# A Mamba scan whose VectorE and GpSimd work goes in pairs of steps, with a new split of the C product between the two

## The chip, the cores and the metric

One core of a Trainium2 chip runs the whole program. The metric is the device time of one execution in microseconds (us), median of the runs. TensorE (PE) multiplies matrices, VectorE (DVE) and GpSimd (POOL) work element by element, ScalarE (ACT) computes activation functions, and SyncE (SP) issues DMAs. Each engine takes its own instructions in program order and waits for the others by semaphores.

## The reference

16 sequences (images cut into 196 patches, and 128 text tokens: L = 324 tokens of H = 192 channels) go through 16 Mamba layers and then through a mixture of 16 experts. The layers are what the change touches:

```python
def mamba_layer(x, p):
    in_w, cw, cb, xp_w, dtw, dtb, a_log, dp, ow, nw = p
    h = rmsnorm(x, nw)
    xz = jnp.einsum('blh,ch->blc', h, in_w)
    u, z = jnp.split(xz, 2, axis=-1)
    u = jax.nn.silu(causal_conv(u, cw, cb))
    proj = jnp.einsum('bli,ci->blc', u, xp_w)
    dt_r, Bm, Cm = (proj[..., :R], proj[..., R:R + N], proj[..., R + N:])
    dt = jax.nn.softplus(jnp.einsum('blr,ir->bli', dt_r, dtw) + dtb)
    A = -jnp.exp(a_log)
    y = selective_scan(u, dt, A, Bm, Cm, dp)   # h = exp(dt*A)*h + dt*u*B;  y = sum over n of h*C, + u*D
    y = y * jax.nn.silu(z)
    return x + jnp.einsum('bli,hi->blh', y, ow)
```

I = 384 channels times N = 16 states give 6144 recurrences over 324 tokens for each sequence and layer.

## The kernel before

A *unit* is one sequence in one layer: 256 units (`UNITS`). A unit's recurrences are cut into 16 *steps* `s`. A step holds 128 partitions times 3 tiles of 324 tokens: 972 elements in each partition. For each step

- ACT writes the decay exp(dt*A) into PSUM (`se_decay`, L646, three instructions, one for each tile). There are two decay buffers, so the decay of step s waits for the scan of step s-2;
- POOL writes dt*u*B into `dbu` (`ge_dbu`, L912), a ring of 4 (`DRING`), so this waits for the scan of step s-4;
- DVE scans (`ve_scan`, L847) into `h`, a ring of 8 (`RING`), so a scan waits for TensorE's sums of the step eight before;
- DVE multiplies `h` by C in place (`ve_product`, L856), which TensorE has spread over the partitions in PSUM (`te_bcast`, L466, once for four steps, one buffer); for the steps in `ON_POOL` = 3, 7 and 12 POOL does it (`ge_product`, L920), from a copy of C in SBUF;
- TensorE sums over the states into `y_ps` (`te_sum`, L479, for two steps at a time).

When the sums of a unit are there, DVE multiplies `y_ps` by silu(z) (`ve_gate`, L864), and TensorE projects the result (`te_out`, L523 and L525). Around this lie, for units further on, the norm (`te_ss` L569, `se_log_ss` L715, `ge_x_norm` L926), the projections (`te_u` L543, `te_z` L508), the convolution (`te_conv` L557), silu (`se_silu` L697 and L703), and dt: `te_dt` L586, then a softplus made of Abs, Relu, Exp, Ln and Identity on ACT and three accumulating DMAs that POOL issues (`ge_dt`, L936 and L940). dt and dt*u go through HBM and come back spread over partitions (`sp_load_dt`, `sp_load_dtu`). All of TensorE's results except the sums and C go through one PSUM bank, `pj`: a projection waits until ACT has copied the one before it out of the bank.

The order of the work is written by hand, one function for each engine (`tensor_step`, `scalar_step`, `vector_step`, `gpsimd_step`, `sync_step`), which stands in a loop of two units. A name such as S5 stands below for the scan of step 5, D5 for its decay and S0' for the scan of step 0 of the next unit.

Of the kernel before, what the change touches and what calls it, by code (L numbers as in the profile page):

```python
# [331 lines left out]

def run_layers(nc, cst, x_T, params, weights, b_rows, dt_rows, dtu_rows):

    ident, ones96, sel_c, fold = cst["ident"], cst["ones96"], cst["sel_c"], cst["fold"]
    with ExitStack() as ctx:
# [110 lines left out]

        def by_vector(u, s):

            if s < 0:
                return by_vector(u - 1, s + N)
            return (N - len(ON_POOL)) * u + sum(i not in ON_POOL for i in range(s + 1)) + 1

        def by_pool(u, s):

            if s < 0:
                return by_pool(u - 1, s + N)
            return len(ON_POOL) * u + sum(i in ON_POOL for i in range(s + 1)) + 1
# [1656 lines left out]
```

## Time and profile before

| | us |
|---|---|
| median of 3 runs | 13945.11 |
| lowest and highest | 13933.89, 13954.32 |
| span of the profiled execution | 13964.1 |
| of it the 256 units | about 12,494 |
| a unit, from one wait of DVE to the next | 48.81 |
| busy in the span: PE, DVE, ACT, POOL | 12204.2, 12892.4, 11365.0, 12631.1 |

The profiled execution's span is its own device time, 19 us (0.14%) above the median. Busy times of DVE and POOL add up records that overlap by a little, since an instruction is recorded as started while the last one's end is still being written; the distance from one start to the next is the real price in a full queue. TensorE's ends are modelled.

### The profile page before, as it was taken

Reading aid. Unit: us, or ns where it says so; the run is one execution under the profiler, and the core shown is the slowest. Engines: PE = TensorE matmul, PEld = TensorE weight load, DVE = VectorE, ACT = ScalarE, POOL = GpSimd, SP = SyncE. Lnnn points to the kernel's source line nnn. Section 1 sums busy time; section 2 is a strip of 40 time slices with the busy share of each in tenths; the row PEclk is TensorE's granted clock in tenths of the full one; section 3 lists DMA queues with packets and bytes.
Section 4 is the critical chain, followed back from the end, with each engine's and each line's share of the span. In section 5 each row is a group of like instructions: output and inputs, shape, how many; then the busy total and the mean of one; then the engine's idle time right before and its main releaser. Section 6 shows DMA issues by size and latency. Waiting matters only on the chain. (4 is left out here: it accounts for less than half of the span.)

```text
span 13964.1 us, 203073 instructions
## 1 busy us (share of the span) xinstructions
PE 12204.2 (87%) x51466; PEld 6379.1 (46%) x51466; DVE 12892.4 (92%) x8757; ACT 11365.0 (81%) x21744; POOL 12631.1 (90%) x6352
## 2 busy tenths in 40 slices
PE   7888888888888888888888888888888888888898
PEld 4444444444444444444444444444444444444776
DVE  2999999999999999999999999999999999997533
ACT  4888888888888888888888888888888888887111
POOL 2999999999999999999999999999999999996033
PEclk8999999999999999999999999999999999999899
DMA  4555555555555555555555555555555555554122
GB/s 104 156 160 157 156 164 161 166 154 161 157 161 161 162 161 155 162 156 165 160 165 155 159 159 156 166 161 163 155 161 156 163 161 161 161 155 128 36 63 52
DMA packets 825576, 2086.15 MB, mean 149 GB/s; under 512 B 101243, under 2 KB 381308, under 8 KB 825336
## 3 DMA queue, kind: packets, MB, share of 16 engines
q1 hardware_dynamic: 693720, 1684.45, 36.0%
q0 software_dynamic: 130992, 399.73, 15.2%
q14 instruction: 114, 0.93, 0.0%
q10 hardware_dynamic: 720, 0.55, 0.0%
q8 instruction: 30, 0.49, 0.0%
HBM read 1414.20 MB, written 286.41 MB: 122 GB/s over the span
## 5 line engine op out<-in xcount | busy, mean ns | idle before, releaser
L912 POOL TENSOR_TENSOR dbu<-dtu_rep,b_rep 128x972 f32<-128x972 f32 x4096 | 9534.2, 2511 | 137.2 <-DVE h L847 109.5
L847 DVE TENSOR_TENSOR_SCAN h<-ps,dbu 128x972 f32<-128x972 f32 x4096 | 8723.4, 2166 | 207.8 <-ACT ps L646 207.8
L646 ACT ACTIVATE ps<-dt_rep,A_cur 128x323 f32<-128x323 f32 x12288 | 5842.5, 520 | 957.0 <-DVE h L847 950.5
L856 DVE TENSOR_TENSOR h<-h,ps 128x972 f32<-128x972 f32 x3329 | 3731.2, 1146 | 0.2 <-DVE ps L1206 0.2
L479 PE MATMUL ps<-h,fold 128*32 128x486 f32 x16400 | 3567.5, 577 | 90.1 <-DVE h L856 89.4
L920 POOL TENSOR_TENSOR h<-h,c_rep 128x972 f32<-128x972 f32 x769 | 1853.0, 2410 | 0.0
L557 PE MATMUL ps<-u_raw,w_cv 128*128 128x162 f32 (+7 forms) x8256 | 1801.5, 372 | 28.6 <-ACT u_raw L682 1.5
L479 PEld LDWEIGHTS ps<-h,fold 128*32 128x32 f32 x16400 | 784.9, 110 | 1961.1 <-issue 1731.1
L557 PEld LDWEIGHTS ps<-u_raw,w_cv 128*128 128x128 f32 x8256 | 1351.6, 190 | 509.4 <-ACT u_pre L689 159.5
L543 PE MATMUL ps<-x_norm,w_u 96*128 96x324 f32 (+1 forms) x4128 | 987.7, 383 | 65.1 <-ACT u_raw L682 55.9
L466 PE MATMUL ps<-c_rows,sel_c 16*128 16x324 f32 x2048 | 827.8, 484 | 209.1 <-DVE h L856 201.2
L508 PE MATMUL ps<-x_norm,w_z 96*128 96x324 f32 (+1 forms) x4112 | 983.5, 383 | 1.4 <-ACT rstd L715 0.7
L525 PE MATMUL ps<-y_gated,w_o 128*96 128x324 f32 x3084 | 925.9, 436 | 0.0
L543 PEld LDWEIGHTS ps<-x_norm,w_u 96*128 96x128 f32 x4128 | 665.7, 191 | 541.1 <-ACT u_raw L682 277.9
L586 PE MATMUL ps<-xp_rows,w_dt 49*128 49x162 f32 (+1 forms) x2064 | 562.1, 393 | 388.7 <-ACT dt L743 207.8
L577 PE MATMUL ps<-u_act,w_x 128*128 128x324 f32 x1548 | 490.2, 453 | 461.8 <-ACT u_act L697 454.8
...
L508 PEld LDWEIGHTS ps<-x_norm,w_z 96*128 96x128 f32 x4112 | 661.1, 190 | 447.0 <-issue 179.5
L466 PEld LDWEIGHTS ps<-c_rows,sel_c 16*128 16x128 f32 x2048 | 299.9, 183 | 834.6 <-DVE h L856 629.8
L586 PEld LDWEIGHTS ps<-xp_rows,w_dt 49*128 49x128 f32 x2064 | 321.0, 187 | 788.0 <-ACT dt L743 429.6
L523 PE MATMUL ps<-x_T,ident 96*96 x1028 | 401.9, 473 | 315.8 <-ACT z_pre L670 201.9
L525 PEld LDWEIGHTS ps<-y_gated,w_o 128*96 128x96 f32 x3084 | 504.5, 164 | 337.0
...
## 6 DMA issues: line engine op xcount, KB each, us to landing
dt_rep<-dt_rows SPq DMA_DIRECT2D x1028, 486.0 KB, 5.6
dtu_rep<-dtu_rows SPq DMA_DIRECT2D x1028, 486.0 KB, 4.8
b_rep<-b_rows SPq DMA_DIRECT2D x1028, 162.0 KB, 5.2
dt<-exp_x POOLq DMA_DIRECT2D x257, 486.0 KB, 5.1
dt<-dtu POOLq DMA_DIRECT2D x257, 486.0 KB, 4.4
dt<-u_pre POOLq DMA_DIRECT2D x257, 486.0 KB, 4.4
dt_rows<-dt SPq DMA_DIRECT2D x257, 486.0 KB, 2.6
dtu_rows<-dtu SPq DMA_DIRECT2D x257, 486.0 KB, 2.6
```

What stands on the lines that cost most here:

```text
L466: pe.matmul(c_ps, sel_c[64:80, q, :], c_rows[par][64:80, :], start=True, stop=True).then_inc(s_cbc, 1)
L479: mm = pe.matmul(y_ps[32 * r:32 * r + 32, half, :], fold[:, :], src[:, half * YW:(half + 1) * YW], start=(m in (0, 1)), stop=(m < 0))
L508: mm = pe.matmul(pj[:, lo:hi], w_z[:, c, it * 128:it * 128 + 128], x_norm[par][:, c, t:t + hi - lo], start=(c == 0), stop=(c == 1))
L525: mm = pe.matmul(pj[0:HC, 0:L], w_o[:, it, half * HC:(half + 1) * HC], y_gated[:, it, :], start=False, stop=(it == IT - 1))
L543: mm = pe.matmul(pj[:, lo:hi], w_u[:, c, it * 128:it * 128 + 128], x_norm[par][:, c, t:t + hi - lo], start=(c == 0), stop=(c == 1))
L557: mm = pe.matmul(pj[:, lo + skip:hi], w_cv[:, it * KC + KC - 1 - back, :], u_raw[:, it * L + t + skip - back:it * L + t + hi - lo - back], ...
L586: mm = pe.matmul(pj[:, lo:hi], w_dt[:, it * 128:it * 128 + 128], xp_rows[0:RB, t:t + hi - lo], start=True, stop=True)
L646: ins = act.activation(decay[s % 2][:, it * L + 1:(it + 1) * L], dt_rep[:, s % NR, it, 1:L], ACT.Exp, scale=A_cur[:, it * N + s:it * N + s ...
L847: dve.tensor_tensor_scan(h[s % RING][:, :, :].rearrange("p i t -> p (i t)"), decay[s % 2], dbu[s % DRING][:, :, :].rearrange("p i t -> p ( ...
L856: dve.tensor_tensor(h[s % RING][:, :, :], h[s % RING][:, :, :], c_ps.unsqueeze(1).broadcast_to([128, IT, L]), ALU.mult).then_inc(s_prod, 1)
L912: pool.tensor_tensor(dbu[s % DRING][:, :, :], dtu_rep[:, r, :, :], b_rep[:, q, :].unsqueeze(1).broadcast_to([128, IT, L]), ALU.mult).then_ ...
L920: pool.tensor_tensor(h[s % RING][:, :, :], h[s % RING][:, :, :], c_rep[:, at, :].unsqueeze(1).broadcast_to([128, IT, L]), ALU.mult).then_i ...
```

## The change

Steps go in pairs. POOL writes `dbu` of two steps by one instruction, and a product with C is one instruction for two steps. POOL now has the product of steps 2 and 3, and of the pair 10 and 11 it takes the first four of the six tiles, while DVE takes the last two; DVE has all other pairs. Each engine's order is written anew, the gate comes behind S1' and waits for all eight sums of its unit, and the pass runs up to five units ahead where it was three. The first memsets of `h`, `z_act` and others go.

```diff
--- before.py
+++ after.py
...
-ON_POOL = (3, 7, 12)
...
-MAIN_SET = "exp_and_others"
+MAIN_SET = "natural_log_exp_and_others"
 LOG_SET = "natural_log"
-FREED = 2 + RING + 1 + 1 + 2 + 1 + 1
+SILU_SET = "silu_and_others"
+FREED = 2
+
+
+DEEP = 5
+
+EXPS = (0, 1, 2, 3, 4, 5, 6, 7, 8, 9, 10, 11, 12, 13, 14, 15)
+SCANS = (0, 1, 2, 3, 4, 5, 6, 7, 8, 9, 10, 11, 12, 13, 14, 15)
+INPUTS = (0, 2, 4, 6, 8, 10, 12, 14)
+PRODUCTS = (0, 4, 6, 8, 10, 12, 14)
+POOL_PRODUCTS = (2, 10)
+SUMS = (0, 2, 4, 6, 8, 10, 14, 12)
+
+ALONE = ()
+SUMMED = 2
+
+SHARED = {10: 4}
+
+
+def turn(order, u, s):
+
+    if s < 0:
+        return turn(order, u - 1, s + N)
+    return len(order) * u + order.index(s) + 1
+
+
+def both(order, u, s):
+
+    if s < 0:
+        return both(order, u - 1, s + N)
+    return turn(order, u, max(s, s + 1, key=order.index))
...
-        def te_sum(pe, u, m):
-
-            reached(pe, s_prod, by_vector(u, 2 * m + 1))
-            if not {2 * m % N, (2 * m + 1) % N}.isdisjoint(ON_POOL):
-                reached(pe, s_pprod, by_pool(u, 2 * m + 1))
-            if m == 0:
-                reached(pe, s_gate, u + 1)
+        def te_sum(pe, u, s):
+
+            if any(at in PRODUCTS for at in range(s, s + SUMMED)):
+                reached(pe, s_prod, turn(PRODUCTS, u, last(PRODUCTS, range(s, s + SUMMED))))
+            if any(at in POOL_PRODUCTS for at in range(s, s + SUMMED)):
+                reached(pe, s_pprod, turn(POOL_PRODUCTS, u, last(POOL_PRODUCTS, range(s, s + SUMMED))))
+            if s < NR:
+                reached(pe, s_gate, u)
             for half in range(2):
-                for s in (2 * m, 2 * m + 1):
-                    r = s % NR
-                    src = h[s % RING][:, :, :].rearrange("p i t -> p (i t)")
-                    mm = pe.matmul(y_ps[32 * r:32 * r + 32, half, :], fold[:, :], src[:, half * YW:(half + 1) * YW],
-                                   start=(m in (0, 1)), stop=(m < 0))
+                for step in range(s, s + SUMMED):
+                    r = step % NR
+                    mm = pe.matmul(y_ps[32 * r:32 * r + 32, half, :], fold[:, :],
+                                   flat(h, step)[:, half * YW:(half + 1) * YW], start=(s < NR),
+                                   stop=(s == last(SUMS, range(s % NR, N, NR))))
             mm.then_inc(s_sum, 1)
...
+                freed = te_dt(pe, v[2], 0, freed)
+            if on[0]:
+                te_sum(pe, v[0], 8)
+            if on[4]:
+                freed = te_ss(pe, v[4], freed)
+            if on[2]:
+                freed = te_dt(pe, v[2], 1, freed)
+            if on[0]:
+                te_sum(pe, v[0], 10)
+            if on[2]:
+                freed = te_z(pe, v[2], q[2], 0, freed)
+            if on[0]:
+                te_sum(pe, v[0], 14)
+            if on[2]:
+                freed = te_z(pe, v[2], q[2], 1, freed)
+            if on[0]:
+                te_sum(pe, v[0], 12)
+                freed = te_out(pe, v[0], 0, freed)
+            if on[1]:
+                te_bcast(pe, v[1], q[1], 0)
+            if on[0]:
+                freed = te_out(pe, v[0], 1, freed)
+            if on[3]:
+                freed = te_u(pe, v[3], q[3], 0, freed)
...
+        def scalar_step(act, u, par):
...
+                se_decay(act, v[0], 12)
+            act.preload_act_table_set(SILU_SET)
+            if on[2]:
+                se_silu_u(act, v[2], q[2])
+            act.preload_act_table_set(MAIN_SET)
+            if on[0]:
+                se_decay(act, v[0], 13)
+            if on[2]:
+                se_xp(act, v[2])
+            if on[0]:
+                se_decay(act, v[0], 14)
+            if on[2]:
+                se_dt(act, v[2], 0)
+            if on[0]:
+                se_decay(act, v[0], 15)
+            if on[1]:
+                se_copy_A(act, v[1])
+            if on[4]:
+                se_log_ss(act, v[4])
+            if on[1]:
+                se_decay(act, v[1], 0)
+            if on[4]:
+                se_copy_nw(act, v[4])
+            if on[2]:
+                se_dt(act, v[2], 1)
+            if on[1]:
+                se_decay(act, v[1], 1)
+            if on[2]:
+                se_exp_x(act, v[2])
+                se_one_plus(act, v[2])
+                se_log(act, v[2])
+                se_z(act, v[2], 0)
+                se_less(act, v[2])
+            if on[1]:
+                se_decay(act, v[1], 2)
+            if on[2]:
+                se_z(act, v[2], 1)
+            if on[3]:
+                se_copy_cb(act, v[3])
+            if on[1]:
+                se_decay(act, v[1], 3)
+            if on[5]:
+                se_sq(act, v[5])
+            if on[1]:
+                se_decay(act, v[1], 4)
+            if on[0]:
+                se_out(act, v[0], 0)
+            if on[2]:
+                se_c_rows(act, v[2], q[2])
+                se_lost(act, v[2])
+            if on[1]:
+                se_decay(act, v[1], 5)
+            if on[0]:
+                se_out(act, v[0], 1)
+            if on[1]:
+                se_decay(act, v[1], 6)
...
         def ve_scan(dve, u, s):
-            reached(dve, s_exp, 16 * u + s + 1)
-            reached(dve, s_dbu, 16 * u + s + 1)
-            if s % 2 == 0:
-                reached(dve, s_sum, 8 * u + s // 2 - 1)
-            dve.tensor_tensor_scan(h[s % RING][:, :, :].rearrange("p i t -> p (i t)"), decay[s % 2],
-                                   dbu[s % DRING][:, :, :].rearrange("p i t -> p (i t)"),
-                                   0.0, ALU.mult, ALU.add).then_inc(s_scan, 1)
+            reached(dve, s_exp, turn(EXPS, u, s))
+            reached(dve, s_dbu, turn(INPUTS, u, s // 2 * 2))
+            reached(dve, s_sum, turn(SUMS, u, s // SUMMED * SUMMED - RING))
+            dve.tensor_tensor_scan(flat(h, s), decay[s % 2], flat(dbu, s), 0.0, ALU.mult, ALU.add).then_inc(s_scan, 1)
 
         def ve_product(dve, u, s):
 
-            if s == min(i for i in range(s // 4 * 4, N) if i not in ON_POOL):
-                reached(dve, s_cbc, 4 * u + s // 4 + 1)
-            reached(dve, s_scan, 16 * u + s + 1)
-            dve.tensor_tensor(h[s % RING][:, :, :], h[s % RING][:, :, :],
-                              c_ps.unsqueeze(1).broadcast_to([128, IT, L]), ALU.mult).then_inc(s_prod, 1)
+            reached(dve, s_cbc, 4 * u + s // NR + 1)
+            n = width(s)
+            reached(dve, s_scan, turn(SCANS, u, last(SCANS, range(s, s + n))))
+            mine = slice(SHARED.get(s, 0), n * IT)
+            dve.tensor_tensor(steps(h, s, n)[:, mine, :], steps(h, s, n)[:, mine, :],
+                              each(c_ps, n)[:, mine, :], ALU.mult).then_inc(s_prod, 1)
 
         def ve_gate(dve, u, par):
 
-            reached(dve, s_sum, 8 * u + 2)
-            reached(dve, s_za, u)
+            reached(dve, s_sum, turn(SUMS, u, SUMS[-1]))
+            reached(dve, s_skip, u + 1)
+            reached(dve, s_za, u + 1)
...
+        def vector_step(dve, u, par):
+
+            v, q, on = pass_of(u, par)
+            if on[0]:
+                ve_scan(dve, v[0], 5)
+                ve_scan(dve, v[0], 6)
+                ve_scan(dve, v[0], 7)
+                ve_product(dve, v[0], 4)
+                ve_product(dve, v[0], 6)
+                ve_scan(dve, v[0], 8)
+                ve_scan(dve, v[0], 9)
+                ve_scan(dve, v[0], 10)
+                ve_scan(dve, v[0], 11)
+                ve_product(dve, v[0], 8)
+                ve_product(dve, v[0], 10)
+                ve_scan(dve, v[0], 12)
+                ve_scan(dve, v[0], 13)
+                ve_scan(dve, v[0], 14)
+                ve_scan(dve, v[0], 15)
+                ve_product(dve, v[0], 12)
+                ve_product(dve, v[0], 14)
+            if on[1]:
+                ve_scan(dve, v[1], 0)
+                ve_scan(dve, v[1], 1)
+            if on[0]:
+                ve_gate(dve, v[0], q[0])
+            if on[1]:
+                ve_scan(dve, v[1], 2)
+                ve_scan(dve, v[1], 3)
+                ve_scan(dve, v[1], 4)
+                ve_product(dve, v[1], 0)
...
-            reached(pool, s_scan, 16 * u + s + 1 - DRING)
-            pool.tensor_tensor(dbu[s % DRING][:, :, :], dtu_rep[:, r, :, :],
-                               b_rep[:, q, :].unsqueeze(1).broadcast_to([128, IT, L]), ALU.mult).then_inc(s_dbu, 1)
+            reached(pool, s_scan, both(SCANS, u, s - DRING))
+            pool.tensor_tensor(steps(dbu, s, 2), steps(dtu_rep, r, 2), each(b_rep[:, q, :], 2), ALU.mult).then_inc(s_dbu, 1)
...
+            at = POOL_PRODUCTS.index(s)
+            wait(pool, s_cr[at], 16 * (u + 1))
+            n = width(s)
+            reached(pool, s_scan, turn(SCANS, u, last(SCANS, range(s, s + n))))
+            mine = slice(0, SHARED.get(s, n * IT))
+            pool.tensor_tensor(steps(h, s, n)[:, mine, :], steps(h, s, n)[:, mine, :],
+                               each(c_rep[:, at, :], n)[:, mine, :], ALU.mult).then_inc(s_pprod, 1)
...
+        def gpsimd_step(pool, u, par):
+
+            v, q, on = pass_of(u, par)
+            if on[0]:
+                ge_product(pool, v[0], 2)
+            if on[1]:
+                ge_add(pool, v[1], 2)
+            if on[0]:
+                ge_dbu(pool, v[0], 8)
+                ge_dbu(pool, v[0], 10)
+            if on[1]:
+                ge_dtu(pool, v[1], q[1])
+            if on[0]:
+                ge_dbu(pool, v[0], 12)
+                ge_dbu(pool, v[0], 14)
+            if on[3]:
+                ge_x_norm(pool, v[3], q[3])
+            if on[0]:
+                ge_product(pool, v[0], 10)
+            if on[1]:
+                ge_dbu(pool, v[1], 0)
+                ge_dbu(pool, v[1], 2)
+            if on[2]:
+                ge_add(pool, v[2], 0)
+            if on[1]:
+                ge_dbu(pool, v[1], 4)
+            if on[2]:
+                ge_add(pool, v[2], 1)
+            if on[1]:
+                ge_dbu(pool, v[1], 6)
...
+        def sync_step(sp, u, par, due=()):
...
+                sp_load_dtu(sp, v[1], 0)
+                sp_load_dt(sp, v[1], 0)
+                sp_load_dtu(sp, v[1], 1)
+                sp_load_dt(sp, v[1], 1)
+            if on[2]:
+                sp_store_b(sp, v[2], q[2])
+            if on[1]:
+                sp_load_dtu(sp, v[1], 3)
+                sp_load_dt(sp, v[1], 2)
+                sp_load_c(sp, v[1], q[1], 0)
+                sp_load_dtu(sp, v[1], 2)
...
```

How the order of instructions changes is shown at two places. The first is on TensorE (PE), around the last sums of a unit. L479 (now L528) is `te_sum`, L508 (now L560) `te_z`, L466 `te_bcast`, and L523 (now L571) is the start of `te_out`. Before:

```order
L466 MATMUL ps<-c_rows,sel_c 128x324 [waits s_prod]
L62 ISA
L508 MATMUL ps<-x_norm,w_z 128x324 [waits s_lnss,s_wz]
L508 MATMUL ps<-x_norm,w_z 128x324
L508 MATMUL ps<-x_norm,w_z 128x162 x2
L479 MATMUL ps<-h,fold 32x486 [waits s_prod]
L479 MATMUL ps<-h,fold 32x486 x3
L79 ISA
L508 MATMUL ps<-x_norm,w_z 128x162 [waits s_zev]
L508 MATMUL ps<-x_norm,w_z 128x162
L508 MATMUL ps<-x_norm,w_z 128x324 x2
L62 ISA [waits s_gate]
```

Now, on TensorE at the same place:

```order
L78 REGISTER_ALU
L528 MATMUL ps<-h,fold 32x486 [waits s_prod]
L528 MATMUL ps<-h,fold 32x486 x3
L560 MATMUL ps<-x_norm,w_z 128x162 [waits s_zev]
L560 MATMUL ps<-x_norm,w_z 128x162
L560 MATMUL ps<-x_norm,w_z 128x324 x2
L78 REGISTER_ALU
L528 MATMUL ps<-h,fold 32x486 [waits s_prod]
L528 MATMUL ps<-h,fold 32x486 x3
L571 ISA [waits s_wo,s_gate,s_zev]
L571 MATMUL ps<-x_T,ident 96x324
L573 MATMUL ps<-y_gated,w_o 96x324 x3
```

Before, the unit's last sum (L479) stood ahead of the second half of z and was the last thing that the gate needed. Now two sums stand on the two sides of that half: steps 14 and 15 first, then z, then steps 12 and 13, and both are needed by the gate.

The second place is on GpSimd (POOL), around the product of the middle pair. L912 (now L997) is `ge_dbu`, L920 (now L1006) the product, L926 (now L949) the norm, L940 `dtu`. Before:

```order
L926 TENSOR_TENSOR x_norm<-x_norm,rstd 96x648 [waits s_xw,s_rstd]
L79 REGISTER_ALU
L912 TENSOR_TENSOR dbu<-dtu_rep,b_rep 128x972 [waits s_scan]
L79 REGISTER_ALU
L912 TENSOR_TENSOR dbu<-dtu_rep,b_rep 128x972 [waits s_scan]
L62 ISA
L79 REGISTER_ALU [waits s_acc]
L940 TENSOR_TENSOR dtu<-dt,u_act 128x972 [waits s_ua]
L920 TENSOR_TENSOR h<-h,c_rep 128x972 [waits s_scan,s_cr1]
L79 REGISTER_ALU [waits s_bq3]
L912 TENSOR_TENSOR dbu<-dtu_rep,b_rep 128x972 [waits s_scan]
```

Now, on GpSimd:

```order
L949 TENSOR_TENSOR x_norm<-x_norm,rstd 96x648 [waits s_xw,s_rstd]
L1006 TENSOR_TENSOR h<-h,c_rep 128x1296 [waits s_scan,s_cr1]
L61 ISA
L78 REGISTER_ALU [waits s_bq0,s_dur1,s_dur0]
L997 TENSOR_TENSOR dbu<-dtu_rep,b_rep 128x1944 [waits s_scan]
L78 REGISTER_ALU [waits s_dur3,s_dur2]
L997 TENSOR_TENSOR dbu<-dtu_rep,b_rep 128x1944 [waits s_scan]
L78 REGISTER_ALU
L78 ISA [waits s_less]
L61 ISA [waits s_dtev]
L1017 DMA dt<-exp_x 128x972 [waits s_acc]
```

Every `dbu` instruction now holds 1944 elements in a partition instead of 972, waits for the second scan of a pair, and needs two of the replicated `dtu_rep` blocks at once; the shared product (1296 elements) stands right behind the norm.

## Rows read from the trace of the kernel before

**Rows 1.** Windows: PE, PEld, DVE, ACT, POOL busy us; then clock, DMA share, GB/s.

```profile
281.00:12775.00 12494.00, 10952.26 (x45534) 5433.33 (x45534) 12355.49 (x7669) 11032.55 (x20981) 12353.44 (x6139) 1.00 0.54 160
5999.54:6048.35 48.81, 42.78 (x180) 21.25 (x178) 48.33 (x31) 43.13 (x83) 48.32 (x25) 1.00 0.53 158
...
12790.00:12794.00 4.00, 2.79 (x10) 0.65 (x12) 3.31 (x4) 0.00 (x0) 0.00 (x0) 0.73 1.01 350
```

**Rows 2.** The timeline of DVE in a unit: start, length, and idle time before.

```profile
5999.54 6.33 DVE L847 TENSOR_TENSOR_SCAN h<-ps,dbu 128x972 f32<-128x972 f32 x3 [0.48 <-ACT ps L646]
6005.79 3.29 DVE L856 TENSOR_TENSOR h<-h,ps 128x972 f32<-128x972 f32 x3
6009.00 4.25 DVE L847 TENSOR_TENSOR_SCAN h<-ps,dbu 128x972 f32<-128x972 f32 x2
...
6014.22 1.16 DVE L864 TENSOR_TENSOR y_gated<-ps,z_act 128x972 f32<-128x972 f32 x1
6015.30 2.17 DVE L847 TENSOR_TENSOR_SCAN h<-ps,dbu 128x972 f32<-128x972 f32 x1
```

**Rows 3.** The timeline of POOL in the same unit.

```profile
6017.55 2.25 POOL L912 TENSOR_TENSOR dbu<-dtu_rep,b_rep 128x972 f32<-128x972 f32 x1 [0.40 <-DVE h L847]
...
6027.94 2.53 POOL L912 TENSOR_TENSOR dbu<-dtu_rep,b_rep 128x972 f32<-128x972 f32 x1
6030.14 1.84 POOL L926 TENSOR_TENSOR x_norm<-x_norm,rstd 96x648 f32<-96x648 f32 x1
...
6040.48 9.07 POOL L912 TENSOR_TENSOR dbu<-dtu_rep,b_rep 128x972 f32<-128x972 f32 x4
6049.32 2.43 POOL L920 TENSOR_TENSOR h<-h,c_rep 128x972 f32<-128x972 f32 x1
6051.52 6.85 POOL L912 TENSOR_TENSOR dbu<-dtu_rep,b_rep 128x972 f32<-128x972 f32 x3
```

**Rows 4.** The timeline of ACT in the same unit.

```profile
6000.81 0.56 ACT L742 ACTIVATE exp_x<-ps 128x486 f32<-128x486 f32 x1
...
6001.76 1.44 ACT L646 ACTIVATE ps<-dt_rep,A_cur 128x323 f32<-128x323 f32 x3
...
6004.18 1.01 ACT L749 ACTIVATE exp_x<-exp_x 128x972 f32<-128x972 f32 x1
6005.10 2.79 ACT L646 ACTIVATE ps<-dt_rep,A_cur 128x323 f32<-128x323 f32 x6
6007.91 1.28 ACT L778 ACT_TABLE_LOAD   x1
...
6009.64 1.09 ACT L753 ACTIVATE dtu<-exp_x,one 128x972 f32<-128x972 f32 x1
...
6019.28 1.11 ACT L757 ACTIVATE u_pre<-exp_x,one 128x972 f32<-128x972 f32 x1
...
6042.72 1.48 ACT L697 ACTIVATE u_act<-u_pre,cb_cur 128x324 f32<-128x324 f32 x3
```

**Rows 5.** The page's DMA issues: size of one and us to landing.

```profile
dtu_rep<-dtu_rows SPq DMA_DIRECT2D x1028, 486.0 KB, 4.8
```

**Rows 6.** The timeline of PE around the sums ahead of the gate.

```profile
6005.39 1.33 PE L569 MATMUL ps<-sq,ones 96*96 96x324 f32 x4
...
6009.14 0.81 PE L466 MATMUL ps<-c_rows,sel_c 16*128 16x324 f32 x2 [0.25 <-DVE h L856]
6009.88 1.90 PE L508 MATMUL ps<-x_norm,w_z 96*128 96x324 f32 x8
6011.71 1.82 PE L479 MATMUL ps<-h,fold 128*32 128x486 f32 x8
6013.47 1.91 PE L508 MATMUL ps<-x_norm,w_z 96*128 96x162 f32 x8
```

**Rows 7.** The last unit's end: sums on PE, the gate on DVE.

```profile
12791.21 4.88 PE L479 MATMUL ps<-h,fold 128*32 128x486 f32 x16 [1.53 <-DVE h L856]
...
12796.14 1.17 DVE L864 TENSOR_TENSOR y_gated<-ps,z_act 128x972 f32<-128x972 f32 x1 [2.83 <-PE ps L479]
```

More of the change, by code:

```diff
@@ L325, in _, with width, last, runs @@
                             root((g - 1) * NG + i)
-MAIN_SET = "exp_and_others"
+MAIN_SET = "natural_log_exp_and_others"
 LOG_SET = "natural_log"
-FREED = 2 + RING + 1 + 1 + 2 + 1 + 1
+SILU_SET = "silu_and_others"
[18 more added lines that the diff above has]
+    return turn(order, u, max(s, s + 1, key=order.index))
+def width(s):
+    return 1 if s in ALONE else 2
+def last(order, steps):
+    return max((s for s in order if s in steps), key=order.index)
+def runs(u, ahead):
+    return not isinstance(u, int) or u + ahead >= 0
 def run_layers(nc, cst, x_T, params, weights, b_rows, dt_rows, dtu_rows):
@@ L446, in pick, with flat, steps, each @@
             return table[:, la * width:(la + 1) * width] if isinstance(la, int) else table[:, bass.ds(la * width, width)]
[L449 to L459, printed above, removed]
+        def flat(ring, s):
+            return ring[:, s % ring.shape[1], :, :].rearrange("p i t -> p (i t)")
+        def steps(ring, s, n):
+            at = s % ring.shape[1]
+            return ring[:, at:at + n, :, :].rearrange("p s i t -> p (s i) t")
+        def each(rows, n):
+            return rows.unsqueeze(1).broadcast_to([128, n * IT, L])
         def te_bcast(pe, u, par, q):
@@ new lines, in se_exp_x, with se_log, se_one_plus @@
+        def se_exp_x(act, p):
+            reached(act, s_dtev, 2 * p + 2)
+            act.activation(exp_x[:, :], exp_x[:, :], ACT.Exp, scale=-1.0).then_inc(s_e, 1)
+        def se_log(act, p):
+            reached(act, s_e, p + 1)
+            wait(act, s_dst[1], 16 * p)
+            act.activation(dtu[:, :], exp_x[:, :], ACT.Ln, bias=cst["one"][:, 0:1]).then_inc(s_l, 1)
+        def se_one_plus(act, p):
+            reached(act, s_e, p + 1)
+            reached(act, s_ua, p + 1)
+            wait(act, s_acc, 48 * p)
+            act.activation(u_pre[:, :], exp_x[:, :], ACT.Identity, bias=cst["one"][:, 0:1]).then_inc(s_one, 1)
@@ L762, in se_c_rows, with se_lost, se_less @@
+        def se_lost(act, p):
+            reached(act, s_one, p + 1)
+            act.activation(u_pre[:, :], u_pre[:, :], ACT.Identity, bias=cst["one"][:, 0:1], scale=-1.0).then_inc(s_lost, 1)
+        def se_less(act, p):
+            reached(act, s_one, p + 1)
+            reached(act, s_l, p + 1)
+            act.activation(exp_x[:, :], exp_x[:, :], ACT.Identity, bias=less[:, 0:1]).then_inc(s_less, 1)
         def se_c_rows(act, p, par):
@@ L1094, in early @@
         def early(step, eng):
-            step(eng, -3, 1, scan=False, a1=False, b1=False)
-            step(eng, -2, 0, scan=False, b1=False)
-            step(eng, -1, 1, scan=False)
+            for u in range(-DEEP, 0):
+                step(eng, u, u % 2)
         def all_units(step, eng):
             early(step, eng)
-            with eng.Fori(0, UNITS // 2) as pair:
+            with eng.Fori(0, UNITS // 2) as two:
                 for par in range(2):
-                    step(eng, 2 * pair + par, par)
+                    step(eng, 2 * two + par, par)
```

689 lines of the change are left out of this document (254 added, 435 removed).

## Prediction

> **What bounds the kernel now.** I read the windows first [rows 1]. The reader should see that two engines are near the top at once: the 256 units take 12,494 us, 48.8 us each, and inside one unit of 48.81 us DVE is busy 48.33, POOL 48.32, ACT 43.13 and PE 42.78, with the granted clock of TensorE at 1.00, its 2.4 GHz level. So the kernel is one long steady state: whatever changes a unit by 0.1 us changes the time by 26 us, and everything before and behind the units is as it was, but for some memsets and the filling of the pipeline.
>
> Then the timelines, for the price of an instruction in a full queue, which is the distance between starts. On DVE [rows 2] three scans take 6005.79 - 5999.54 = 6.25, so a scan (S) is 2.083 us; three products take 6009.00 - 6005.79 = 3.21, so one is 1.07; the gate is 6015.30 - 6014.22 = 1.08. The only wait of DVE in a unit is 0.48, for ACT. On POOL [rows 3] I go by ends: a `dbu` is (6.85 + 6051.52 - 2.43 - 6049.32)/3 = 2.207, say 2.20; the product behind four of them ends 2.20 after them; the norm (648 elements) ends 1.51 after the `dbu` before it. POOL waits 0.40 for a scan; the rest of the unit, 48.81 - 20 x 2.20 - 1.51 - 0.40 = 2.9, is its three DMA issues.
>
> **What the change does to each sum.** DVE: still 16 scans, 33.33 us. 13 products become six of 1944 elements and one of 648. No row shows a product of 1944. With no fixed part a pair is 2 x 1.07 = 2.14; with a fixed part as large as the overlap of records (3.29 - 3.21 = 0.08) it is 2.06. I take 2.06, since every short instruction of the trace costs more for an element than a long one, and 0.73 for the 648 elements. With the gate: 33.33 + 12.36 + 0.73 + 1.08 = 47.50 (47.4 to 47.9), against 48.33. If nothing waited, the unit would be 1.3 us shorter.
>
> POOL: the trace has no instruction of 1944 elements. From 648 and 972 elements, (2.20 - 1.51)/324 = 2.13 ns for an element and 0.13 us fixed; a pair is 4.27, the shared product of 1296 elements 2.89. Sum: eight `dbu` and one product of 4.27, 38.4; 2.89; `dtu` 2.20; norm 1.51; three DMAs 2.9: 47.9 us. The upper end is twice the single price, 4.40, which makes 49.1; the lower one a fixed part of twice the 0.13, a pair of 4.14 and a sum of 46.7. I take 47.9, nearest to the two rows. The Trainium skill (GPSIMD Engine Reference, Performance versus the Vector engine) gives 4497 ns for a two-input `tensor_tensor` of 2048 fp32 elements; by its rule the pair is an estimate of 4.27 and the sum stays under DVE's, and by doubling the row it does not.
>
> ACT: four table loads a unit in the code before (Ln, main, silu, main) and four after; new is one Identity over 972 elements, 1.11 as recorded and, like the other rows, some 0.09 less between starts [rows 4]. 43.1 + 1.0 = 44.1, not the bound by its sum. I price Exp and Ln out of the common set as before; no row shows that set. PE's sum does not change. SP issues the same loads. I walked its queue at about 5 us to landing [rows 5]: the tightest is `dtu_rep` 2, queued behind D14, which lands some 1.5 us before POOL needs it. It costs nothing unless those transfers crowd.
>
> **Where the new order waits.** Now the sums have to be laid beside each other. Call E the recorded end of the product of steps 14 and 15. DVE then does S0' and S1' and would start the gate at E - 0.08 + 2 x 2.083 = E + 4.09. The gate needs all eight sums, and TensorE has behind E: the sum of 14 and 15, the second half of z, the sum of 12 and 13. From [rows 2, 6]: a product's end to PE's start 0.06 (6009.08 to 6009.14), a sum 1.76 (6011.71 to 6013.47), half of z 1.83 (6009.88 to 6011.71), the last sum 1.82 to its end, and 0.05 from there to the gate (12796.09 to 12796.14 [rows 7]). That is 0.06 + 1.76 + 1.83 + 1.82 + 0.05 = 5.52: the gate waits 1.43 us. Before, this wait was nothing, since one sum was left and a product of DVE stood between.
>
> It is longer if the bank `pj` is not free: the second half of z needs ACT's copy of the first. I follow ACT from the end of S10, call it T: D12 to T + 1.47, a table load 1.30, silu of u 1.50, load 1.33, D13 1.39, `xp_rows` 0.43: T + 7.4. D14 1.39, half of dt 0.95, D15 ends at T + 11.2. DVE would be ready for S15 at T + 11.0 (S11, 2.06, 0.73, three scans, less the overlap): a wait of 0.16. PE behind `xp_rows`: half of dt 1.03 (1.08 recorded), a sum 1.76, the norm's sum 1.33 [rows 6], so T + 11.7; then ACT has the norm's Ln 0.45, D0' 1.39, a small copy 0.15, half of dt 0.95, D1' 1.39, Exp 0.93, Identity 1.02, Ln 1.02, the copy of z 0.56: T + 19.6. E is T + 17.32 + 0.16 = T + 17.5, so the copy ends at E + 2.1 and the sum of 14 and 15 at E + 1.8. The gate moves to E + 5.8 and waits 1.7. (Prices of ACT from [rows 4]: six instructions of D in 2.81, so a decay 1.39 to 1.44; a load 1.28 and the gap behind it; half of dt, two copies, 6001.76 - 6000.81 = 0.95, and a single copy half of that; Exp 0.92; Identity and Ln 1.09 to 1.11 recorded. The pieces without a row, the small copies and the norm's Ln, are estimates from these by their size.)
>
> Behind the waiting gate stand S2', S3', S4' and P0', so all of DVE moves by it. POOL's `dbu` of 6 and 7 waits for S3' and moves along, so POOL gets back 1.5 us of idle time and is not the bound; its other deadlines then hold by 0.4 to 0.9 us.
>
> The unit: 47.50 + 0.16 + 1.74 = 49.4 us, 0.6 more than 48.81. Times 256 that is 151 us. The memsets that go (eight of `h` near 1 us each) and a longer filling roughly cancel. 13,964 + 151 = 14,115 for an execution like the profiled one, and 19 less, 14,096, for the median.
>
> **Rivals.** *The gate's chain is hidden and the sums decide.* For it: 1.3 us of DVE's work is really gone, and PE's ends are modelled, so the chain could be shorter. Then POOL's 47.9 plus the 0.4 it waits today is the unit: 48.2, 13,945 - 0.6 x 256 = 13,790. It decides as soon as TensorE delivers the last sum by E + 4.3; against it, the chain is four prices of plain rows, each of which would have to shrink by a quarter. A cut to 48.7 to 48.9 is between the two and would read as no change.
>
> *A pair on POOL costs twice a single.* For it: nothing in the trace shows a pair cheaper. Then the sum is 49.1, `dbu` of 0 and 1 comes 0.3 after S0' could start, and the unit is 49.7: 14,175.
>
> *TensorE's clock falls.* It now waits about 1 us for E. The granted clock was 0.73 in the window at the end, behind a wait of 1.53, so partly at the 1.2 GHz level, and the two sums there took 4.88 with the wait between them, where two take 3.5 in a unit [rows 1, 6, 7]. If the three pieces behind E ran at the lower level, the gate would come 2.5 us later: 14,700. Against it: PE is idle 6 us of each unit today and its clock stays at 1.00.
>
> *The products do not get shorter in pairs* (2.14 each) adds 0.5 us, to 14,220, inside my range.
>
> **Chances.** The forecast 0.60 (its own range 14,010 to 14,200, from a gate wait of 1.4 to 2.0 and the prices of a pair); hidden chain 0.14; in between, no change 0.08; dear POOL pairs 0.13; clock 0.05. A measurement of this kernel tells about 0.2% (28 us, 0.11 us a unit) from no change. Slower is the forecast but for a small part, the dear pairs and the clock: 0.77; within 0.2%: 0.08; faster: 0.15. The range 13,850 to 14,270 leaves out most of the hidden chain and the clock.
>
> **What would show it.** Right: DVE idle about 1.7 us a unit before `y_gated`, released by PE's sum; PE's second half of z starting within 0.4 us of the end of the sum before it; DVE busy near 47.5 a unit with pairs near 2.06 from start to start; POOL pairs near 4.27 and idle 1.5 a unit before a `dbu`, released by DVE. Wrong: idle time of DVE before scans instead, released by POOL or by ACT; a gate that never waits; a granted clock under 1.00 in the layers; a unit under 48.7.

## The result and the profile after

| | us |
|---|---|
| before, in the same session | 13948.92 (13933.89 to 13954.32) |
| changed | 14532.33 (14505.63 to 14537.02) |
| ratio | 1.0417, 95% interval 1.0402 to 1.0431 |
| forecast | 14096, range 13850 to 14270 |
| span of the profiled execution | 14503.8 |

Slower, as forecast, but 436 us above the number and 262 above the range. Of the page of the changed kernel I show the engines, the granted clock and the groups that moved.

```profile
PE 12326.5 (85%) x51460; PEld 6438.0 (44%) x51460; DVE 12770.4 (88%) x7215; ACT 11732.1 (81%) x22046; POOL 12506.1 (86%) x4049
...
PEclk8999999999999999999999999999999999999799
...
L924 DVE TENSOR_TENSOR_SCAN h<-ps,dbu 128x972 f32<-128x972 f32 x4101 | 8683.4, 2162 | 335.5 <-ACT ps L703 294.0
...
L617 PE MATMUL ps<-u_act,w_x 128*128 128x324 f32 x1548 | 640.3, 563 | 517.0 <-ACT u_act L754 510.0
...
L941 DVE TENSOR_TENSOR y_gated<-ps,z_act 128x972 f32<-128x972 f32 x256 | 299.6, 1170 | 557.4 <-PE ps L528 557.4
...
dtu_rep<-dtu_rows SPq DMA_DIRECT2D x1028, 486.0 KB, 6.1
```

The gate waits 557.4/256 = 2.18 us a unit for PE's sums; it waited for none before. The scans wait 335.5 in all, where they waited 207.8. And PE's `te_xp` takes 563 ns a matmul where the same line (L577) of the kernel before takes 453. The windows say why: first the changed kernel over its layers, then two windows of 4 us around the start of `te_xp` (6024.18 and 6536.80), in a unit with a fall and in one without. They answer to [rows 1], with the same columns.

```profile
600.00:12600.00 12000.00, 10196.03 (x41924) 5051.17 (x41924) 11270.39 (x5654) 10464.55 (x19549) 11251.97 (x3534) 0.96 0.50 150
6022.00:6026.00 4.00, 2.04 (x8) 1.29 (x5) 4.00 (x3) 3.96 (x7) 4.00 (x2) 0.81 0.86 260
6535.00:6539.00 4.00, 2.20 (x7) 1.35 (x8) 4.00 (x3) 3.96 (x8) 4.00 (x2) 1.00 0.89 296
```

PE's clock is no longer at 1.00 all the time; it falls to the 1.2 GHz level in some units and not in others. The records of the clock and the starts of S5 give a table (the inner 216 units, from one S5 to the next, here and below):

| stretch at the lower level in the unit | units | mean, us | median, us |
|---|---|---|---|
| none | 81 | 49.73 | 49.54 |
| 3.4 us | 48 | 50.68 | 50.63 |
| 6.8 us or more | 87 | 52.21 | 52.33 |
| all | 216 | 50.94 | 50.63 |

The kernel before had 48.81 us and no such stretch in all its 216. Of the 138 falls 130 come 20 to 24 us behind S5. That is one place in the program: PE has done the sums 4 and 6 and waits for ACT's silu of u, ahead of `te_xp`, the projection of u that gives B, C and the input of dt. PE's timeline, which answers to [rows 6], first of the kernel before (start, length, idle time before and its releaser):

```profile
6044.44 1.90 PE L577 MATMUL ps<-u_act,w_x 128*128 128x324 f32 x6 [1.80 <-ACT u_act L697]
```

and of the changed kernel, a unit without a fall and one with a fall:

```profile
6532.99 1.85 PE L528 MATMUL ps<-h,fold 128*32 128x486 f32 x16
6536.80 1.90 PE L617 MATMUL ps<-u_act,w_x 128*128 128x324 f32 x6 [1.96 <-ACT u_act L754]
6538.62 0.81 PE L515 MATMUL ps<-c_rows,sel_c 16*128 16x324 f32 x2
6539.92 1.09 PE L624 MATMUL ps<-xp_rows,w_dt 128*128 128x324 f32 x4 [0.49 <-ACT xp_rows L789]
...
6484.57 2.93 PE L617 MATMUL ps<-u_act,w_x 128*128 128x324 f32 x6 [2.07 <-ACT u_act L754]
6487.44 1.44 PE L515 MATMUL ps<-c_rows,sel_c 16*128 16x324 f32 x2
6488.81 1.99 PE L624 MATMUL ps<-xp_rows,w_dt 128*128 128x324 f32 x4
6490.73 2.50 PE L528 MATMUL ps<-h,fold 128*32 128x486 f32 x8
```

`te_xp` 2.93 for 1.90, the broadcast of C 1.44 for 0.81, half of dt 1.99 for 1.09. ACT waits for each of these (0.55 and 1.35 us in that unit) with D14 and D15 queued behind, so the scans are late. DVE in the same two units, answering to [rows 2]:

```profile
6537.20 8.57 DVE L924 TENSOR_TENSOR_SCAN h<-ps,dbu 128x972 f32<-128x972 f32 x4
6545.69 4.24 DVE L932 TENSOR_TENSOR h<-h,ps 128x1944 f32<-128x1944 f32 x2
6549.85 4.24 DVE L924 TENSOR_TENSOR_SCAN h<-ps,dbu 128x972 f32<-128x972 f32 x2
6555.84 1.17 DVE L941 TENSOR_TENSOR y_gated<-ps,z_act 128x972 f32<-128x972 f32 x1 [1.74 <-PE ps L528]
...
6489.67 2.18 DVE L924 TENSOR_TENSOR_SCAN h<-ps,dbu 128x972 f32<-128x972 f32 x1 [0.38 <-ACT ps L703]
6493.23 2.18 DVE L924 TENSOR_TENSOR_SCAN h<-ps,dbu 128x972 f32<-128x972 f32 x1 [1.38 <-PE ps L528]
6495.33 4.24 DVE L932 TENSOR_TENSOR h<-h,ps 128x1944 f32<-128x1944 f32 x2
...
6506.29 1.17 DVE L941 TENSOR_TENSOR y_gated<-ps,z_act 128x972 f32<-128x972 f32 x1 [2.56 <-PE ps L528]
```

S14 waits 0.38, S15 1.38, the gate 2.56 for 1.74: 0.38 + 1.38 + 0.82 = 2.6 of the 2.8 between 49.54 and 52.33. (The row puts S15's wait down to PE's sum, which ended last; the sum that S15 needs was long done. It waited for D15, which ACT ended at 6493.20.) In the unit without a fall the forecast can be read off: the gate starts 5.91 behind the product's end (6555.84 - 6549.93), where I had 5.8. PE behind that product, in the same unit:

```profile
6549.99 1.83 PE L528 MATMUL ps<-h,fold 128*32 128x486 f32 x8 [0.67 <-DVE h L932]
6551.87 1.91 PE L560 MATMUL ps<-x_norm,w_z 96*128 96x162 f32 x8
6553.71 1.82 PE L528 MATMUL ps<-h,fold 128*32 128x486 f32 x8
```

The last sum ends at 6555.53, so the gate starts 0.31 behind it.

### The profile page after: what moved, and what is told of

It is laid out like the page before. It is cut to its first block and busy times, and to the rows that moved or that the text cites. A ratio compares the mean times of both kernels' runs of the same rounds, so it can differ in the third digit from the quotient of the medians.

```text
span 14503.8 us, 195321 instructions
## 1 busy us (share of the span) xinstructions
PE 12326.5 (85%) x51460; PEld 6438.0 (44%) x51460; DVE 12770.4 (88%) x7215; ACT 11732.1 (81%) x22046; POOL 12506.1 (86%) x4049
## 5 line engine op out<-in xcount | busy, mean ns | idle before, releaser
L997 POOL TENSOR_TENSOR dbu<-dtu_rep,b_rep 128x1944 f32<-128x1944 f32 x2052 | 9086.2, 4511 | 652.9 <-DVE h L924 306.8
L924 DVE TENSOR_TENSOR_SCAN h<-ps,dbu 128x972 f32<-128x972 f32 x4101 | 8683.4, 2162 | 335.5 <-ACT ps L703 294.0
L932 DVE TENSOR_TENSOR h<-h,ps 128x1944 f32<-128x1944 f32 (+1 forms) x1793 | 3463.5, 1966 | 0.0
L528 PE MATMUL ps<-h,fold 128*32 128x486 f32 x16384 | 3377.5, 590 | 98.6 <-DVE h L932 98.6
L1006 POOL TENSOR_TENSOR h<-h,c_rep 128x1944 f32<-128x1944 f32 (+1 forms) x512 | 1918.2, 3746 | 0.7 <-DMA c_rep<-b_rows 0.7
L528 PEld LDWEIGHTS ps<-h,fold 128*32 128x32 f32 x16384 | 715.9, 111 | 1808.4 <-issue 1665.9
L560 PE MATMUL ps<-x_norm,w_z 96*128 96x324 f32 (+1 forms) x4128 | 991.8, 384 | 109.6 <-ACT z_pre L727 94.0
L617 PE MATMUL ps<-u_act,w_x 128*128 128x324 f32 x1548 | 640.3, 563 | 517.0 <-ACT u_act L754 510.0
L560 PEld LDWEIGHTS ps<-x_norm,w_z 96*128 96x128 f32 x4128 | 665.0, 191 | 666.9 <-ACT z_pre L727 323.0
L571 PE MATMUL ps<-x_T,ident 96*96 x1024 | 406.1, 478 | 603.3 <-issue 442.9
L515 PE MATMUL ps<-c_rows,sel_c 16*128 16x324 f32 x2050 | 906.4, 524 | 0.0
L624 PE MATMUL ps<-xp_rows,w_dt 128*128 128x162 f32 (+1 forms) x2064 | 651.3, 444 | 207.9 <-ACT rstd L771 159.2
L941 DVE TENSOR_TENSOR y_gated<-ps,z_act 128x972 f32<-128x972 f32 x256 | 299.6, 1170 | 557.4 <-PE ps L528 557.4
L617 PEld LDWEIGHTS ps<-u_act,w_x 128*128 128x128 f32 x1548 | 324.6, 223 | 857.9 <-issue 795.2
```

What stands on the lines that cost most here:

```text
L560: mm = pe.matmul(pj[:, lo:hi], w_z[:, c, it * 128:it * 128 + 128], x_norm[par][:, c, t:t + hi - lo], start=(c == 0), stop=(c == 1))
L617: mm = pe.matmul(pj[0:XROWS, 0:L], w_x[:, it, :], u_act[par][:, it, :], start=(it == 0), stop=(it == IT - 1))
L924: dve.tensor_tensor_scan(flat(h, s), decay[s % 2], flat(dbu, s), 0.0, ALU.mult, ALU.add).then_inc(s_scan, 1)
L932: dve.tensor_tensor(steps(h, s, n)[:, mine, :], steps(h, s, n)[:, mine, :], each(c_ps, n)[:, mine, :], ALU.mult).then_inc(s_prod, 1)
L997: pool.tensor_tensor(steps(dbu, s, 2), steps(dtu_rep, r, 2), each(b_rep[:, q, :], 2), ALU.mult).then_inc(s_dbu, 1)
L1006: pool.tensor_tensor(steps(h, s, n)[:, mine, :], steps(h, s, n)[:, mine, :], each(c_rep[:, at, :], n)[:, mine, :], ALU.mult).then_inc(s_pp ...
```

## The experiments

Theory: a fall of PE's clock hangs on the idle stretch ahead of `te_xp`, and the falls are what the forecast missed; under them lies the gate's chain as forecast. Rivals stand in the expectations. A filler is a matmul whose result nobody reads. Every experiment but one changes the changed kernel; times are medians, ratios are to the kernel before on the same chip.

**1. Fill the wait ahead of `te_xp`.**

```diff
+    te_fill(pe, v[2], q[1], freed)   # IT matmuls: w_x on the other unit's u_act, into pj
     freed = te_xp(pe, v[2], q[2], freed)
```

> Three more matmuls on the other unit's u_act, into pj, which the next product overwrites, stand ahead of te_xp and fill most of TensorE's 1.96 us wait for u_act. Theory (the idle stretch ahead of te_xp is what TensorE's clock falls behind, and the falls cost the changed kernel its 1.2 us a unit over the forecast): granted clock 0.99 or more, unit 49.5 us, about 14,150 us. Rival 1 (the falls are a by-product, and the 51 us unit has another cause): clock may rise, unit stays 50.9, 14,530 us. Rival 2 (the clock falls behind another idle stretch then): clock stays 0.96, 14,500 to 14,600 us.

14193.27 us, ratio 1.0176 (1.0155 to 1.0197): 339 us less by giving PE more to do. 204 of 216 units have no fall, the unit is 49.69, the gate still waits 441.7/256 = 1.73.

```profile
600.00:12600.00 12000.00, 10518.25 (x44417) 5295.09 (x44416) 11529.50 (x5795) 10708.34 (x20038) 11530.77 (x3624) 1.00 0.52 154
```

**2. The same amount of filler at another place** (the wait for the gate).

```diff
     te_sum(pe, v[0], 12)
+    te_free(pe, freed)
+    for i in range(3):
+        pe.matmul(pj[0:HC, 0:L], ident[0:HC, 0:HC], x_T[:, 0, cols(v[0])], start=True, stop=True)
     freed = te_out(pe, v[0], 0, freed)
```

> Control for the filler: three matmuls of 0.62 us (the residual's transposition three times, overwritten by the product that follows) stand in the idle time of TensorE behind the last sum, where it waits for the gate, and the 1.96 us wait ahead of te_xp is left as it is. Theory (it is the idle stretch ahead of te_xp that the clock falls behind): falls in about 60% of units as in the changed kernel, unit 50.8 to 51.2, 14,500 to 14,600 us. Rival (any more work of TensorE in a unit stops the falls): clock 1.00, 14,200 us.

14527.27 us, ratio 1.0413 (1.0396 to 1.0431): nothing gained. Falls in 156 of 216 units, all 20 to 24 us behind S5, unit 51.12. So it is not PE's work in a unit that counts, but where it idles.

```profile
600.00:12600.00 12000.00, 10569.63 (x43214) 5265.27 (x43210) 11239.42 (x5637) 10434.61 (x19491) 11219.93 (x3524) 0.96 0.50 150
```

**3. One matmul of filler.** As 1, but only the first matmul.

```diff
-    for it in range(IT):
-        pe.matmul(pj[0:XROWS, 0:L], w_x[:, it, :], u_act[par][:, it, :], start=(it == 0), stop=(it == IT - 1))
+    pe.matmul(pj[0:XROWS, 0:L], w_x[:, 0, :], u_act[par][:, 0, :], start=True, stop=True)
```

> The filler ahead of te_xp is one matmul of 0.62 us in place of three, so the wait for u_act shrinks from 1.96 us to about 1.3 us only. If the fall hangs on the length of that one idle stretch (0 of 216 units fall at 1.80 in the kernel before, 135 at 1.96 in the changed kernel, 114 at 2.9 in the one with a moved sum), the falls go here too: clock 0.98 or more, unit 49.6, 14,170 to 14,220 us, as with three matmuls. Rival (it hangs on how much TensorE has to do around there): falls in a third of the units or more, 14,300 to 14,500 us.

14188.57 us, ratio 1.0175 (1.0158 to 1.0192), no fall in 203 of 216, unit 49.72. PE's timeline there:

```profile
6444.85 0.81 PE L624 MATMUL ps<-u_act,w_x 128*128 128x324 f32 x2
6446.84 1.87 PE L617 MATMUL ps<-u_act,w_x 128*128 128x324 f32 x6 [1.18 <-issue]
```

One matmul, with 1.18 us of idle time left behind it, does as much as three.

**4. The kernel before, with a longer wait at this place.** The sum of steps 6 and 7 goes behind `te_xp`.

```diff
             if scan:
                 te_sum(pe, u, 2)
+            if a1:
+                te_xp(pe, k, par)
+            if scan:
                 te_sum(pe, u, 3)
             if a1:
-                te_xp(pe, k, par)
                 te_dt(pe, k, 0)
```

> The kernel before with one sum (1.8 us of TensorE) moved from ahead of te_xp to behind it, so that TensorE idles some 3.6 us there and not 1.80. Theory (the clock falls behind an idle stretch ahead of te_xp once it is a little longer): the granted clock falls in most units here too, mean under 0.98, and the time rises by 0 to 1.5 us a unit, 13,950 to 14,300 us, by how much VectorE waits. Rival (idle time there has no part in it, it is the whole stream of the changed kernel): clock stays 1.00, time 13,950 us.

14138.45 us, ratio 1.0145 (1.0126 to 1.0164). The wait is 2.90 (I had expected 3.6) and the clock falls in 114 of 216 units, where the kernel before has none; those last 50.29, the other 102 the old 48.81. PE in a unit with a fall and in the next:

```profile
6038.06 3.00 PE L577 MATMUL ps<-u_act,w_x 128*128 128x324 f32 x6 [2.90 <-ACT u_act L699]
...
6088.35 1.90 PE L577 MATMUL ps<-u_act,w_x 128*128 128x324 f32 x6 [2.91 <-ACT u_act L699]
```

**5. Undo the split.** Steps 10 and 11 wholly on DVE; GpSimd's product of them and the load of its C go too.

```diff
-POOL_PRODUCTS = (2, 10)
+POOL_PRODUCTS = (2,)
-SHARED = {10: 4}
+SHARED = {}
```

> Undoes the split: the product of steps 10 and 11 stands wholly on VectorE, steps 2 and 3 stay on GpSimd. VectorE's work rises by 2.06 - 0.73 = 1.33 us to 48.83; the product 14/15 ends 1.33 later, while ScalarE's copy of z does not move, so the gate wait is the row of TensorE alone, 1.43: unit 48.83 + 0.16 + 1.43 = 50.4 us where the clock holds. Theory: the clock falls in most units here too, since the wait for u_act is the same: 14,450 to 14,700 us. Rival (the split itself brings the falls): clock 1.00, 14,370 us.

14576.12 us, ratio 1.0452 (1.0434 to 1.0469). 93 units with no fall have a median of 50.59 (gate wait 1.69 from where the scan before it would have let it start, 1.61 as recorded, not the 1.43 I gave it), the other 123 a mean of 51.54. The falls aren't the split's doing; the split as such saves 50.59 - 49.54 = 1.05 us a unit.

**6. The order of sums**, to take the gate's wait away.

```diff
-SUMS = (0, 2, 4, 6, 8, 10, 14, 12)
+SUMS = (0, 2, 4, 6, 8, 10, 12, 14)
+    te_sum(pe, v[0], 12)
     te_sum(pe, v[0], 14)
     freed = te_z(pe, v[2], q[2], 1, freed)
-    te_sum(pe, v[0], 12)
```

> Sums run in the order 12, 14 and both ahead of the second half of z, so TensorE has two matmul groups of 1.9 us less between the last product and the gate. Theory (gate wait of 1.74 us is TensorE's row of work behind product 14/15): gate wait under 0.5 us in units with no fall, time down by 1.3 to 2.0 us a unit, 14,000 to 14,200 us, the falls of the clock staying. Rival (the gate waits for z's copy on ScalarE and not for TensorE's row): gate wait stays near 1.8, 14,530 us.

14141.08 us, ratio 1.0144 (1.0123 to 1.0165). The gate waits for nothing; the unit is 49.48. Falls now in 211 units, 128 of the 225 falls at 38 us or more behind S5: PE, done sooner, waits up to 1.9 us for ACT's copy of z.

**7. Both, filler and order of sums.**

> Both edits, the filler matmuls and the order of sums. Theory: they add, unit 47.7 to 48.3 us (the 47.50 us of VectorE's own work and small waits), 13,680 to 13,830 us, under the kernel before. Rival: with the gate's wait gone another chain ends last (C products of GpSimd or ScalarE's copies), unit 48.8 or more, 13,950 us or more.

14045.29 us, ratio 1.0073 (1.0053 to 1.0093), unit 49.16: the theory's 47.7 to 48.3 is wrong and the rival's time right, but the chain that now ends last is none of the two it named: it is POOL's `dbu`, which waits for a load. POOL's waits of that kernel (waited for; us in total, times, longest), and its timeline:

```profile
POOL dbu L1005 <- DMA dtu_rep<-dtu_rows: 257.7, 242, 3.1
```
```profile
6089.75 4.33 POOL L1005 TENSOR_TENSOR dbu<-dtu_rep,b_rep 128x1944 f32<-128x1944 f32 x1 [1.27 <-DVE h L932]
6095.32 4.31 POOL L1005 TENSOR_TENSOR dbu<-dtu_rep,b_rep 128x1944 f32<-128x1944 f32 x1 [1.25 <-DMA dtu_rep<-dtu_rows]
```

1.06 us a unit of waiting for `dtu_rep` on top of 47.9 of work is 49.0. (The other wait in these rows, for a scan, comes only 31 times.) The changed kernel has the same wait, 257.1, hidden by the gate's.

**8. The order of loads**, on top of 7.

```diff
+    sp_load_dtu(sp, v[1], 2)
     sp_load_dtu(sp, v[1], 3)
     sp_load_dt(sp, v[1], 2)
     sp_load_c(sp, v[1], q[1], 0)
-    sp_load_dtu(sp, v[1], 2)
```

> The kernel with both edits, and SyncE issues the loads of dtu_rep 2 and 3 ahead of the loads of dt_rep 2 and of C. Theory (the 49.16 us unit of that kernel has GpSimd as its bound: 47.9 us of work and 1.06 us of waiting for dtu_rep): that wait falls under 0.4 us a unit, the unit to 48.2 to 48.6 us, 13,790 to 13,900 us. Rival 1 (the loads land no earlier since they crowd each other or dt_rep 2 comes late for ScalarE's decay 14): unit stays at 49.1, 14,040 us, or rises. Rival 2 (GpSimd's pairs are slowed by VectorE's work, and fill the gap): unit 48.8 to 49.0.

13807.85 us, ratio 0.9896 (0.9880 to 0.9913): faster than the kernel before. The wait is 3.4 in all, the unit 48.26.

```profile
POOL dbu L1005 <- DMA dtu_rep<-dtu_rows: 3.4, 6, 1.1
```

**9. Three tiles of six for POOL**, on top of 8: `SHARED = {10: 3}`.

> The same, and GpSimd takes three of the six tiles of steps 10 and 11, VectorE the other three. GpSimd's sum falls by 0.72 us to 47.2, VectorE's rises by 0.34 to 47.84 and 0.25 of small waits. If GpSimd is the bound of the kernel before this edit, the unit becomes 48.0 to 48.2 us, 13,740 to 13,800 us, under the kernel before; if it is not, the unit rises by 0.3 us.

13818.51 us, ratio 0.9912 (0.9895 to 0.9928), not to be told from 8. Neither case of the expectation (unit 48.24): POOL's listed waits rise from 109.7 to 262.5 us, so it is the bound no longer, and DVE's fall from 87.7 to 63.5, so its 0.34 more of work is in part made up by less waiting.

**10. A second filler**, on top of 8, where the falls now are.

```diff
+    for i in range(2):
+        pe.matmul(ps[0:HC, 6, 0:L], ident[0:HC, 0:HC], x_T[:, 0, cols(v[0])], start=True, stop=True)
     freed = te_out(pe, v[0], 0, freed)
```

> The 13,808 us kernel (filler ahead of te_xp, order of sums, order of loads) has 103 of 216 units in which the clock falls, nearly all 38 to 42 us behind S5, where TensorE waits 1.6 to 1.9 us for ScalarE's copy of z. Two matmuls of 0.62 us (the residual's transposition, into the bank of C, which the next broadcast overwrites) fill 1.24 us of that wait. Theory (each fall stands behind one idle stretch near 2 us): clock 1.00, unit 47.9, 13,700 to 13,730 us. Rival (something else is left that makes the clock fall, or the unit's mean is not made by the falls): clock under 0.99 or unit at 48.2, 13,800 us.

13789.50 us, ratio 0.9892 (0.9875 to 0.9908). The clock is as forecast, no fall in any of 216 units; the time isn't, it is that of 8.

```profile
600.00:12600.00 12000.00, 10833.34 (x46905) 5613.89 (x46904) 11924.74 (x5987) 11064.94 (x20698) 11923.96 (x3742) 1.00 0.53 159
```

In kernel 8 the 81 units with one low stretch of 3.4 us have a median of 47.98, those with none 47.89. In the mean the falls of kernel 8 are worth 48.26 - 48.10 = 0.16 us a unit, 0.34 for each of the 103 units with a fall. So a stretch that costs 1.1 us ahead of `te_xp` (50.63 - 49.54) costs 0.1 by the medians and 0.3 by the means here. ACT waits for PE here too (153.9 us in all for the results of `te_out`, none in kernel 10), but the scans wait only 39.0 us for ACT, where they waited 175.8 in the changed kernel. Kernels 8 and 10 are the fastest of the study, 1.0 and 1.1% under the kernel before.

**11. Both orders, no filler.**

> Only the order of sums and the order of loads, no filler. Theory: the clock falls in nearly every unit (ahead of te_xp and behind the half of z), as in the kernel with the order of sums alone, where that cost 0.3 us against the kernel with filler; the loads take 0.9 us off: unit 48.5 to 48.9, 13,850 to 13,970 us, near the kernel before. Rival (with GpSimd's wait gone the falls cost as much as in the changed kernel, 1.2 us): 14,100 us.

13865.55 us, ratio 0.9942 (0.9926 to 0.9959), unit 48.55; it too beats the kernel before. Falls in 211 of 216 units, but only 24 of them ahead of `te_xp` (where the wait is now 1.73 in the mean), where I had expected both places. Those 24 stand behind waits of 1.86 to 2.65 us; of the 159 waits under 1.80 none has a fall behind it.

**12. The gate one scan later**, PE's order as it was.

```diff
-    ve_gate(dve, v[0], q[0])
     ve_scan(dve, v[1], 2)
+    ve_gate(dve, v[0], q[0])
     ve_scan(dve, v[1], 3)
```

> Only the gate is moved, one scan later (behind S2'), TensorE's order stays. Theory (the gate needs the last sum at E + 5.8 us): VectorE would start it at E + 6.17, the wait goes from 1.8 to 0 in units with no fall; then GpSimd with its wait for dtu_rep is the bound, 48.9 us in such a unit, and with the falls of the clock 49.4 in the mean, 14,130 us, as with the order of sums. Rival (the wait moves along with the gate): 14,500 us.

14350.11 us, ratio 1.0295 (1.0278 to 1.0313). The gate waits for nothing, as the chain to E + 5.8 demands, and units with no fall are 48.65. But PE now idles longer for the later gate (2.3 us in most units, where it was 1.72), and in 147 of 216 units the clock falls there, ahead of `te_out` and the broadcast of C:

```profile
6047.04 1.83 PE L528 MATMUL ps<-h,fold 128*32 128x486 f32 x8
6051.52 1.07 PE L571 MATMUL ps<-x_T,ident 96*96 x2 [2.65 <-issue]
6052.38 3.24 PE L573 MATMUL ps<-y_gated,w_o 128*96 128x324 f32 x6
```

Those units last 51.10; the 14,130 had 49.4 for the mean of all units, which is 50.31.

## Why the prediction was wrong

- **The sum of DVE's work, 47.50, was right.** In a unit with no fall 49.54 - 0.15 - 1.81 (the waits before S13 and the gate, from start to start) = 47.58. A pair from start to start is 2.07 to 2.09 (I took 2.06), the shared product 0.74.
- **The wait of 0.16** is there (0.15), at S13 and not at S15: four scans in 8.57 above.
- **The gate's wait was right in its mechanism, and in its size partly by luck: 1.74 forecast**, 1.81 in units with no fall (the row's 1.74 is counted from the recorded end of S1', 0.08 later). Experiments 6 and 12 take it away from either side, by PE's order and by DVE's. But two terms of it were off and cancel. From the end of the last sum to the gate I had 0.05, from one row at the very end; it is 0.30 in every unit with no fall. The wait for the bank `pj` was to add 0.3; the second half of z starts 1.94 behind E (6551.87 - 6549.93) and 1.81 in experiment 5, so it adds 0.13. My sum for it was also 0.2 too long: 7.4 + 1.03 + 1.76 + 1.33 is 11.5, not 11.7. With 1.43 + 0.25 + 0.13 the wait is 1.81, and without the copy it is the 1.69 of experiment 5. The forecast unit of 49.4 is the 49.54 of 81 units.
- **The rivals but the clock are refuted.** The hidden chain: the gate waits. The dear pairs on POOL: in the unit without a fall two pairs behind `dtu` end 8.52 after it (6531.93 to 6540.45), 4.26 each (4.27 forecast). POOL's sum of 47.9 was not under DVE's 47.50, as the prediction has it, but only under DVE's unit with its waits.
- **The step that failed is the rival on TensorE's clock.** I gave it 0.05, put it behind E, and set against it that PE is idle 6 us of a unit and keeps its clock. The falls came some 13 us earlier, ahead of `te_xp`, behind a wait that the kernel before already had at 1.80 us and that I did not look at; it is 1.96 or 2.07 now. The sum of idle time does not tell: experiments 1 and 2 take some 1.9 us from it at two places, and the first takes away nearly all falls, the second none. What PE does in that one wait decides, as experiments 1, 3 and 4 show. The missing term is 50.94 - 49.73 = 1.21 us a unit, 310 us; experiment 1 gives 339 of the 436 by the medians of the runs, and 308 between the profiled executions, from which the 1.21 comes (that of the changed kernel is its fastest run, 27 us under the median). Of the rest, (49.73 - 49.4) x 256 = 84 is in units with no fall, more than half of it in a few long ones.
- **`dtu_rep` 2 costs nothing:** true for the changed kernel, for a wrong reason. I had it land 1.5 us early with 4.8 us to landing [rows 5]; it took 6.1 and POOL waited 257.1 us in 236 units, 1.09 each, behind the gate's longer wait. It became the bound in experiment 7.
- **Slower at 0.77** held, by its own mechanism: with falls in only 12 units of 216 the kernel is still 1.8% slower (experiment 1).

Open: what decides whether a wait brings a fall. Ahead of `te_xp` the kernel before waits 1.82 us at most and has no fall. In the changed kernel the two units of a pass differ: of the waits of 1.95 or 1.96 us 49 of 103 have a fall behind them, of those of 2.06 to 2.10 81 of 106, of the seven of 1.49 to 1.60 none. At this place no fall of any kernel here stands behind a wait under 1.86. But length alone does not decide: 2.90 us gives a fall in only 114 of 216 units (experiment 4), and ahead of `te_out`, 38 to 42 us behind S5, kernel 8 has 102 falls behind waits of 1.62 to 1.93 us, while the changed kernel, whose waits there are 1.72 to 1.77, has 7 in its 216 units. What else counts isn't settled. The Trainium skill (TensorE: Matmul & The Clock Gate, HAM oscillation) has such falls in a kernel whose waits are 3 to 5 us; the waits here are shorter, 1.6 to 2.9, and the clock falls.
